# A fused mLSTM cross-attention and MX feed-forward kernel: the weight chain turned by two units against the batches, and the first half tile of the FFN in other PSUM banks

## The reference, cut to what matters

```python
def _L0_xattn_ref(q, k, v, Wi, bi, Wf, bf, ln_scale):      # 8 batches, 256 positions, 16 heads of 32
    ...
    D = jnp.exp(log_D - max_log_D)
    qk = jnp.einsum('bhsd,bhtd->bhst', qh, kh) / sqrt(dh)
    C = qk * D
    normalizer = jnp.maximum(jnp.abs(C.sum(-1, keepdims=True)), jnp.exp(-max_log_D))
    h = jnp.einsum('bhst,bhtd->bhsd', C / (normalizer + EPS), vh)
    hn = (h - mu) * jax.lax.rsqrt(var + EPS) * ln_scale    # per head
def _L0_ffn_ref(x, w_gate, w_up, w_down):                  # every operand of a product rounded in blocks of 32
    gate = _mx_linear(x, w_gate)
    up = _mx_linear(x, w_up)
    return _mx_linear(silu(gate) * up, w_down)
x = x + _L0_xattn_ref(_layernorm(x), ctx, ctx, Wi, bi, Wf, bf, ln_scale)
x = x + _L0_ffn_ref(_layernorm(x), w_gate, w_up, w_down)
```

## Time and profile before

| | |
|---|---|
| median of 3 runs | 545.32 us (544.28 to 547.44) |
| profiled execution | 548.92 us, of which 547.0 us is the span of the trace |
| busy in the span | PE 449.5, DVE 434.3, POOL 249.9, ACT 243.2 us |
| mixer, from 109.86 us (first `c_mult`) to 334.89 us (first `gate`) | DVE starts the eight batches at 109.86, 130.90, 160.69, 190.92, 221.13, 251.59, 281.97 and 312.81 us |
| FFN, from 334.89 us | first `pair` at 341.38, last at 531.16 us |
| granted PE clock | mean 0.877 of full speed |

### The profile page before, as it was taken

One profiled execution on the slowest core, in us unless ns is written; L12 is line 12 of the kernel. 1 busy time (PEld: TensorE's weight loads), 2 busy tenths in 40 slices (PEclk: granted clock), 3 DMA queues, 4 the chain that ended last, 5 costly groups with the idle time before them and its releaser, 6 DMA issues.

```text
span 547.0 us, 10343 instructions
## 1 busy us (share of the span) xinstructions
PE 449.5 (82%) x3465; PEld 299.6 (55%) x3465; DVE 434.3 (79%) x615; ACT 243.2 (44%) x341; POOL 249.9 (46%) x228
## 2 busy tenths in 40 slices
PE   0697988399778686959789698799799999999993
PEld 0597988168556465657658384344344444444441
DVE  5569886679798897979789876798978888888781
ACT  1656663246354363726264464244344434434431
POOL 2444541232553537264644564755334353354443
PEclk9997885579978797987859577799989999999999
DMA  7455621143231413141420203011111111111211
GB/s 225 155 185 168 224 98 38 42 120 116 84 114 59 140 59 120 24 146 48 131 67 20 77 2 116 1 38 40 38 40 40 68 47 38 38 38 39 76 38 38
DMA packets 30566, 43.73 MB, mean 80 GB/s; under 512 B 6980, under 2 KB 11972, under 8 KB 30532
## 3 DMA queue, kind: packets, MB, share of 16 engines
q1 hardware_dynamic: 27280, 42.80, 23.8%
q10 hardware_dynamic: 3252, 0.46, 0.5%
HBM read 34.41 MB, written 8.85 MB: 79 GB/s over the span
## 4 chain that ended last, share of the span: by engine, by line
PE 42%; issue 18%; POOL 17%; DVE 13%; ACT 4%; DMA 3%; POOLq 1%; SPq 0%; DVEq 0%; ACTq 0%
PE psA L1359 8%; PE psA L1368 8%; PE psC L1386 7%; PE psC L1193 4%; POOL early L615 3%; PE psB L1378 3%; PE psA L1256 2%; PE psC L1236 2%; DMA early<-in_x_dram 2%; POOL wq L552 2%; POOL kTa L678 2%; POOL xc L648 2%; PE psA L1165 2%; DVE qTa L1128 2%; DVE pam L941 2%
## 5 line engine op out<-in xcount | busy, mean ns | idle before, releaser
L678 POOL TENSOR_TENSOR kTa<-kTa,ps 128x1024 bf16<-128x1024 bf16 x32 | 62.0, 1937 | 100.8 <-DVE kTa L1131 100.8
L1284 PE MATMUL psA<-vp,DC 128*128 128x128 f32 x512 | 72.4, 309 | 12.1 <-DVE DC L1035 12.1
L1284 PEld LDWEIGHTS psA<-vp,DC 128*128 128x128 f32 x512 | 70.1, 223 | 14.1 <-issue 14.1
L552 POOL TENSOR_TENSOR wq<-wq,ws 128x1024 bf16<-128x1024 bf16 x24 | 50.6, 2108 | 51.9 <-DVE wq L969 51.9
L1359 PE MATMUL psA<-WgT,qTa 128*128 128x512 bf16 x256 | 64.7, 399 | 2.5 <-ACT hf L823 2.5
L1368 PE MATMUL psA<-WuT,qTa 128*128 128x512 bf16 x256 | 63.1, 391 | 1.2 <-DVE kTa L1119 1.2
L1386 PE MATMUL psC<-WdT,kTa 128*128 128x512 bf16 x256 | 60.5, 379 | 2.4 <-ACT kTa L888 2.4
L888 ACT ACTIVATE kTa<-psB 128x1024 bf16<-128x1024 bf16 x32 | 32.8, 1024 | 58.1 <-PE psB L1378 57.9
L1119 DVE TENSOR_TENSOR kTa<-kTa,psA 128x1024 f32<-128x1024 f32 x32 | 39.0, 1219 | 19.4 <-PE psA L1368 19.4
L1035 DVE SCALAR_TENSOR_TENSOR DC<-psA,DC 128x512 f32<-128x512 f32 x64 | 41.0, 684 | 13.5 <-ACT DC L814 10.7
L814 ACT ACTIVATE DC<-psB 128x512 f32<-128x512 f32 x64 | 37.2, 597 | 20.1 <-PE psB L1270 19.6
(11 more groups left out here) (132 smaller groups left out, 857.8 us busy)
## 6 DMA issues: line engine op xcount, KB each, us to landing
early<-in_x_dram SPq DMA_DIRECT2D x16, 512.0 KB, 4.0
wraw<-in_L_ffn_w_down_dram SPq DMA_DIRECT2D x8, 512.0 KB, 5.6
early<-in_ctx_dram SPq DMA_DIRECT2D x8, 512.0 KB, 4.8
wraw<-in_L_ffn_w_gate_dram SPq DMA_DIRECT2D x8, 512.0 KB, 4.3
wraw<-in_L_ffn_w_up_dram SPq DMA_DIRECT2D x8, 512.0 KB, 3.4
x_scratch<-early SPq DMA_DIRECT2D x8, 512.0 KB, 3.0
kTa<-x_scratch SPq DMA_DIRECT2D x16, 256.0 KB, 2.7
out_dram<-kTa SPq DMA_DIRECT2D x16, 256.0 KB, 2.0
```

The lines of the kernel that those rows point to most:

```text
L552: nc.gpsimd.tensor_tensor(blocks(wq[p][:, :]), blocks(wq[p][:, :]), spread(ws4[p][:, :], UB), ALU.mult).then_inc(wq_ready.sem, 1)
L678: nc.gpsimd.tensor_tensor(blocks(pd[h]), blocks(pc[h]), spread(ps4[h][:, :], PB), ALU.mult).then_inc(pq_ready.sem, 1)
L1284: last = nc.tensor.matmul(psA[:, j, to:to + P], DC[n % DCN][:, i4 * P:(i4 + 1) * P], values[:, left:left + P], start=i4 == 0, stop=c == 0, ...
```

## The change

In the code a weight unit w has its number: 8 and 9 are the first gate and up unit, and so on to 23.

1. The weight chain is shifted. DVE does `w_front` of unit 10 and `w_round` of unit 9 before the first batch. In each step its list becomes `c_mult` x4, `head_var`, `w_pow`(2b+10), `w_front`(2b+11), `head_norm`, `w_round`(2b+10), `c_mult` x4, `x1_stats`, `w_pow`(2b+11), `w_front`(2b+12), `w_round`(2b+11), `x1_round`. ACT, POOL, PE and SP follow: `round_const` of the second unit now stands ahead of `copy_h` of the second chunk, `x1_norm` behind it and behind two `exps`; POOL does `w_back` first, `carry_q` later; PE's two `w_transpose` stand behind the decays.
2. The end of the mixer. The last step has no `x1_round(6)` and no x1_norm(6); both, with `head_var(7)`, go into the first FFN tiles, and `x1_round` is split into three (`x1_amax`, `x1_scale`, `x1_clamp`) that stand between different half tiles. POOL's `last_power` is split in two and its `residual` into `layer_scale` and `residual`, also between half tiles.
3. The first half tile goes to psB and psC: `gate` and `up` of (0, 0) need not wait for psA to be emptied. In tile 1 `gate` goes ahead of `p_transpose`. The activation table is loaded ahead of `copy_h`.
4. The last half tile is worked in two halves: POOL scales one and DVE the other, PE transposes them into two banks, ACT copies one and DVE the other, and DVE does the last product-and-sum straight from PSUM.
5. Before the mixer PE does the transposes of the gates ahead of those of the last w_down unit.

```diff
@@ SP, turn @@
+                if weights:
+                    sp.wait_ge(y_ready.sem, y_ready.unit(2 * b + B + 2))
+                    settle(sp)
+                    load_gate(b + 2)
...
@@ POOL, step and the FFN's start @@
             def step(b, p, n, first, last):
+                w_back(2 * b + B + 1, 1)
                 if not first:
                     head_rsqrt(b - 1)
-                if not first:
+                    layer_scale(b - 1)
                     residual(b - 1)
                 if not last:
-                    carry_q(b + 1, 1 - p)
-                w_back(2 * b + B + 1, 1)
+                    w_back(2 * b + B + 2, 0)
                 if not first:
                     x1_rsqrt(b - 1)
                 if not last:
-                    w_back(2 * b + B + 2, 0)
+                    carry_q(b + 1, 1 - p)
                     weigh(b + 1, 1 - p)
-                if not first:
+                if not (first or last):
                     back_x(b - 1)
...
-            last_power(B - 1)
             back_p(0, 0)
             back_p(0, 1)
-            residual(B - 1)
+            last_power(B - 1, 0)
             back_p(1, 0)
+            last_power(B - 1, 1)
             back_p(1, 1)
             add_x1(0, 0, 0)
-            x1_rsqrt(B - 1)
             back_p(2, 0)
             back_p(2, 1)
             add_x1(1, 1, 0)
+            layer_scale(B - 1)
             back_p(3, 0)
-            back_x(B - 1)
+            residual(B - 1)
             back_p(3, 1)
+            back_x(B - 2)
             add_x1(2, 0, 1)
...
@@ ACT, step @@
                 copy_h(b, p, 0)
                 exps(b, 4)
                 exps(b, 5)
+                if not last:
+                    round_const(2 * b + B + 2, 0)
+                evac_gate_up(2 * b + B + 1, 1, b)
                 copy_v(b, p, 1)
...
-                if not first:
-                    x1_norm(b - 1)
+                if last:
+                    act.preload_act_table_set("silu_and_others")
+                else:
+                    round_const(2 * b + B + 3, 1)
                 copy_h(b, p, 1)
-                evac_gate_up(2 * b + B + 1, 1, b)
-                if not last:
+                if last:
+                    silu(0, 0, first=True)
+                else:
                     exps(b + 1, 0)
                     exps(b + 1, 1)
+                    if not first:
+                        x1_norm(b - 1)
...
@@ DVE, step and the FFN's start @@
                 if not last:
-                    w_front(2 * b + B + 2, 0, b + B // 2 + 1)
-                w_round(2 * b + B + 1, 1)
+                    w_pow(2 * b + B + 2, 0)
+                    w_front(2 * b + B + 3, 1, b + B // 2 + 1)
                 if not first:
                     head_norm(b - 1, 1 - p)
+                if not last:
+                    w_round(2 * b + B + 2, 0)
                 for k in range(HPC, 2 * HPC):
                     c_mult(b, k)
...
-            pair(0, 0)
+            pair(0, 0, first=True)
             pair(0, 1)
-            head_norm(B - 1, 1)
+            head_var(B - 1, 1)
             pair(1, 0)
             pair(1, 1)
+            x1_amax(B - 2, fch)
+            pair(2, 0)
+            head_norm(B - 1, 1)
+            pair(2, 1)
+            x1_scale(B - 2, fch)
+            pair(3, 0)
+            x1_clamp(B - 2)
+            pair(3, 1)
+            pair(4, 0)
             x1_stats(B - 1)
...
@@ PE, the FFN's first half tile @@
+            def first_half():
+                pe.wait_ge(d_exp.sem, d_exp.at(B - 1, 8))
+                for a in range(PC):
+                    for c in range(HC):
+                        last = nc.tensor.matmul(psB[a][:, :], xqT[0][:, 0, c * P:(c + 1) * P], WgT[:, c, a * E:(a + 1) * E],
+                                                start=c == 0, stop=c == HC - 1)
...
@@ DVE, the last half tile @@
+                if last_one:
+                    nc.vector.tensor_scalar(pc[h][:, tail[0]], p8[:, tail[0]], ACT_MAX, -ACT_MAX, ALU.min,
+                                            ALU.max).then_inc(tail_q, 1)
...
+            def tail_end(t):
+                nc.vector.tensor_tensor(blocks(pd[1][:, tail[1]]), blocks(pc[1][:, tail[1]]),
+                                        spread(ps4[1][:, tail_b[1]], PB // 2), ALU.mult).then_inc(tail_back[1], 1)
...
+                nc.vector.tensor_copy(pTs[1][:, tail[1]], psA[:, 0, :].bitcast(BF16)[:, tail[1]]).then_inc(tail_ev[1], 1)
...
+                nc.vector.scalar_tensor_tensor(out=yo[1], in0=psC[1][:, :], scalar=(W_OUT * A_OUT) ** 2, in1=x1r[1],
+                                               op0=ALU.mult, op1=ALU.add).then_inc(y_out.sem, 1)
```

More of the change, by code:

```diff
@@ L1028, in _ @@
             w_pow(B + 1, 1)
+            w_front(B + 2, 0, B // 2 + 1)
+            w_round(B + 1, 1)
             ch = Chain(ve, dve_step, 2 * DVE_LINKS)
@@ L1084, in x1_round @@
                                         ALU.max).then_inc(xc_ready.sem, 1)
+            def x1_round(b):
+                x1_amax(b, ch)
+                x1_scale(b, ch)
+                x1_clamp(b)
             def step(b, p, n, first, last):
+                more = not (isinstance(b, int) and b >= B - 2)
                 for k in range(HPC):
@@ L1146, in _ @@
+            pair(3, 0)
+            x1_clamp(B - 2)
+            pair(3, 1)
+            pair(4, 0)
+            x1_stats(B - 1)
+            pair(4, 1)
+            pair(5, 0)
+            pair(5, 1)
+            x1_amax(B - 1, fch)
+            pair(6, 0)
+            x1_scale(B - 1, fch)
+            pair(6, 1)
+            x1_clamp(B - 1)
+            pair(7, 0)
+            pair(7, 1)
+            with ve.Fori(0, TILES // 2 - 5) as i:
                 fch.enter(i)
@@ L1398, in tile @@
                         x_transpose(moved)
                     down(t - 1, 1 - q, h)
+            first_half()
             pe.wait_ge(h_ev.sem, h_ev.at(B - 1, 2))
[L1402 to L1409 removed]
+            gate(0, 0, 0, 1, free=True)
@@ L1410, in _ @@
+            up(0, 0, 0, 1, free=True)
+            tile(1, 0, 1, second=True)
+            for t in range(2, 10):
+                tile(t, t // 2, t % 2, moved={5: B - 2, 9: B - 1}.get(t))
             pe.wait_ge(xqT_ev.sem, xqT_ev.at(B - 1, 1))
-            with pe.Fori(0, TILES // 2 - 3) as i:
+            with pe.Fori(0, TILES // 2 - 5) as i:
                 for p in range(2):
-                    tile(2 * i + 6 + p, i + 3, p)
-            for h in range(2):
-                p_transpose(TILES - 1, h)
-                down(TILES - 1, 1, h)
+                    tile(2 * i + 10 + p, i + 5, p)
```

243 lines of the change are left out of this document (152 added, 91 removed).

## The result

The changed kernel takes 554.09 us (552.77 to 557.16, 4 runs) against 545.86 us of the kernel before (4 runs): ratio 1.0153, 95% interval 1.0121 to 1.0186. It is 8.2 us slower. The profiled execution took 552.83 us, of which 550.8 us is the span.

A forecast was written before the change was run, and what follows sets the result against it. DVE was taken as nearest the limit in the mixer, PE in the FFN. Steps +7.5, start +0.2, entry +2.1, tail -3.4 made +6.4 on the profiled execution; median forecast 551.5 us (chance 0.45), range 534 to 559.

The forecast's parts named there:

- The gap: DVE in a mixer step, before `x1_stats`: idle 2.25 us becomes a blocked 2.15, `x1_stats` starting at 18.05 (before 17.9).
- The size of a step: Mixer step: 30.9 to 31.8 us instead of 30.3; +1.25 taken, +7.5 over six steps, bounds +3 and +10.
- (b): DVE after `x1_stats` in a mixer step: `carry_q` meets `w_front` or `w_round`, 1.25 us, and `w_round` ends at 27.0.
- fourth rival: Mixer and FFN entry: PE stays at its lower clock, +1.7 us a step and +5, 558 us; chance 0.13.
- Before the mixer and step 0: Added `w_front` and `w_round` (3.0 + 2.4 us) fit DVE's 5.53 us wait for first exponents: 0 to +1, +0.2 taken.
- The entry: Start of the FFN, to pair 16: 6.9 us gained, 9.0 given back, so +2.1; bounds -5 and +5.
- first rival: Mixer slower, but FFN entry gains 4 to 5 us as moved pieces mostly fit into waits: about 545; chance 0.17.
- The tail: Last clamp's start to end of last sum: 8.85 us becomes about 5.4, gain 3.4 (2.5 to 4.2).
- Sum: Whole kernel: +7.5 + 0.2 + 2.1 - 3.4 = +6.4 us on the profiled execution of 548.9.
- the second: Mixer: DVE's idle time does take `w_round`, step about 29.1 us, -7; total 535, or 530 with entry kept; chance 0.10.
- The third: Mixer steps stay at 30.3 us, later `x1_norm` hidden by DVE's queue; FFN entry gains 5: 537; chance 0.15.

## Why the prediction was right, step by step

The forecast was +6.4 on the profiled execution and 551.5 us; the median is 554.1, inside the range of 534 to 559, and slower, as forecast. The mechanism was right too. The sizes were less good, and that the total is near has some luck in it: the mixer cost 3.5 us more than forecast and the tail gained 1.1 less, while the entry cost 2.3 less.

- **The gap (right).** Forecast: `x1_stats` as before, an idle 2.25 us turned into a blocked 2.15. The step above has `x1_stats` at 17.6 without idle time, `w_round` 3.16 instead of 1.22, `head_norm` ending at 10.9 (11.1), L622 held by L1006. The second `c_mult` group starts at 15.2 (15.6), `inter` at 21.4 (21.65), `x1_norm` ends at 27.2 (27.5), `w_round` at 26.2 (27.0). The run without the conflict shows that it is the cause: 2.9 us a step, with `x1_norm` late.
- **The size of a step (mis-sized: +1.25 taken, +1.82 measured).** The prediction gave the heads 5.22 us at the lower clock. Behind waits of 3.4, 2.8, 3.4, 2.7, 3.2 and 3.4 us they took 6.5, 5.4, 6.6, 5.4, 5.2 and 6.6 us, and the steps 32.5, 31.9, 32.8, 31.7, 31.3 and 32.6: long heads, long step. The prediction's own figures for cold heads, `x1_norm` at 27.5 and then 4.25, come to 31.75 us, +1.45; it took a value between warm and cold heads, and in no step were they warm. The rest is the heads of 6.5 us and more. Its term (b), DVE's own queue, does not set the end: the sixth of these steps has no `w_front` behind `x1_stats` and is among the longest. That the late `x1_norm` sets it is shown by moving that line: back to 30.22, where DVE's list is next. So six steps cost 11.0 instead of 7.5, a little more than the +1.7 a step of the fourth rival.
- **Before the mixer and step 0 (right, as far as it can be told).** The profile pair has -5.9 and +1.1, but the start varies from 103.9 to 112.0 us with the same instructions ahead of it. Over the eight profiles with the added `w_front` and `w_round` it is 107.9 on average, over the five of the old order 107.3; +0.2 was forecast, and a spread of 8 us can't confirm it.
- **The entry (mechanism right, +2.1 forecast, -0.2 measured).** First pair at 21.7 as forecast, `pair(1, 0)` at 35.8 (36.2). Then the blocks cost 5.5 instead of 7.0, and the clock was better than before: 0.97 from 334 to 450 us, against 0.93 from 334.89 to 443.89. How much the clock gave is not shown. The 6.9 us gained are given back whole, so the first rival's kept 4 to 5 us did not come.
- **The tail (-3.4 forecast, -2.3 measured).** From the last clamp's start to the end it takes 5.7 us (5.4 forecast, before 8.85). What was missed lies ahead of the clamp: `add_x1` of the tile before now stands ahead of POOL's half product and meets the last pair, whose L987 takes 1.12 instead of 0.18. It is a step moved past another on POOL's queue, and the prediction did not count it.
- **Sum.** 11.0 - 0.2 - 2.3 make 8.5 without the start and step 0, for which no size is shown; the medians say 8.2. Of what the profile was to show, two figures just missed: the steps are 32.14 apart on average (31 to 32 forecast, three of the six above), and pair 16 came at 130.9 (131 to 135).

The rivals: the second holds under its condition only. The third had a late `x1_norm` hidden by DVE's queue, and that did not happen; its 30.3 us a step came only when `x1_norm` was moved ahead. The fourth was at work in the steps' long heads, but not in the entry, where it had +5; its own terms add up to 557.3 rather than 558. What stays open is what makes the clock fall in one step and not in the next.

## What to carry to other kernels

An idle gap on DVE that ends with a POOL step is free only for operations that do not meet POOL: move a block maximum into it, not a product of two SBUF operands. Even then the gain came only after ACT's list had been put in order, two runs later. Whatever a later engine's list holds behind the moved work must be checked too; here one ACT operation behind `copy_h` and two exponents cost 1.9 us a step, where the gap had held 2.25. Where the moved work makes PE wait longer, look at the clock of what follows: behind waits of 2.7 to 3.5 us the heads here took 5.2 to 6.6 us instead of 3.8, and not the same from step to step.
